# Two-layer transformer block on one core: scores from split bf16 operands against fp32 scores on 32-row groups of TensorE

## Time and profile before

| | us |
|---|---|
| median of three runs | 294.47 (289.23 to 296.59) |
| the profiled execution | 290.26 |
| its span on the core | 288.4 |
| PE busy | 208.4 (72%) |
| DVE busy | 187.2 (65%) |
| ACT busy | 118.9 (41%) |
| POOL busy | 83.0 (29%) |
| mean granted clock of TensorE | 0.846 of 2.4 GHz |

### The profile page before, as it was taken

How to read it: one execution, slowest core, us unless ns; L and a number is a source line. 1 busy time by engine, 2 the same in 40 slices (tenths; PEclk the granted TensorE clock), 3 DMA queues, 4 the chain that set the end, 5 groups by cost and what they waited for, 6 DMA issues and landing times.

```text
span 288.4 us, 4749 instructions
## 1 busy us (share of the span) xinstructions
PE 208.4 (72%) x1541; PEld 153.4 (53%) x1541; DVE 187.2 (65%) x545; ACT 118.9 (41%) x265; POOL 83.0 (29%) x110
## 2 busy tenths in 40 slices
PE   2812776745978697948878797866985978782996
PEld 1512654624757466736557575543764755261683
DVE  4656875148885885488776945678578566715763
ACT  2510565516576361325783622353563421341220
POOL 1402675328054321123371312050512021001000
PEclk9965599765699999795899997978699999586699
DMA  4562712204001210220002200200020002000000
GB/s 118 173 159 74 273 39 65 52 16 92 2 4 46 71 50 0 50 61 0 3 18 64 64 18 0 56 18 2 4 53 5 0 2 60 16 4 0 0 0 18
DMA packets 21895, 12.61 MB, mean 44 GB/s; under 512 B 2966, under 2 KB 20998, under 8 KB 21878
## 3 DMA queue, kind: packets, MB, share of 16 engines
q1 hardware_dynamic: 20790, 11.88, 15.3%
q10 hardware_dynamic: 1088, 0.52, 0.7%
HBM read 5.44 MB, written 0.54 MB: 21 GB/s over the span
## 4 chain that ended last, share of the span: by engine, by line
PE 34%; DVE 27%; issue 14%; POOL 7%; ACT 6%; DMA 5%; SPq 5%; DVEq 0%; POOLq 0%; ACTq 0%
PE bank L1104 6%; PE bank L1124 5%; PE bank L1059 5%; DVE mx L731 3%; DVE xn L709 3%; POOL rstd L372 3%; PE bank L1045 3%; ACT pt L551 3%; POOL es L413 3%; DVE ct L750 3%; SPq L255 2%; SPq L258 2%; DVE es L721 2%; PE bank L1013 2%; DVE stats L697 2%
## 5 line engine op out<-in xcount | busy, mean ns | idle before, releaser
L413 POOL TENSOR_TENSOR es<-es,mx 128x512 f32<-128x512 f32 x32 | 33.3, 1053 | 38.5 <-DVE mx L716 38.1
L1034 PE MATMUL bank<-ident,es 128*128 128x128 f32 x128 | 25.2, 345 | 10.4 <-ACT es L539 10.2
L372 POOL TENSOR_TENSOR rstd<-ve,half 128x2 f32<-128x2 f32 x16 | 11.2, 698 | 67.7 <-DVE ve L703 67.3
L539 ACT ACTIVATE es<-es 128x512 f32<-128x512 f32 x32 | 19.0, 626 | 27.4 <-POOL es L413 27.3
L583 ACT ACTIVATE gth<-bank 128x256 f32<-128x256 f32 (+1 forms) x36 | 13.4, 380 | 37.7 <-PE bank L1104 37.7
L1034 PEld LDWEIGHTS bank<-ident,es 128*128 128x128 f32 x128 | 19.1, 179 | 14.2 <-ACT es L539 13.7
L1104 PE MATMUL bank<-xnT,wg 128*128 128x256 f32 (+1 forms) x72 | 25.7, 441 | 0.6 <-DVE gb L836 0.4
L721 DVE TENSOR_TENSOR es<-bank,biasq 128x512 f32<-128x512 f32 x32 | 21.2, 684 | 7.5 <-PE bank L1018 7.4
L1059 PE MATMUL bank<-pt,va 128*32 128x128 f32 x512 | 25.0, 292 | 0.0
L830 DVE SCALAR_TENSOR_TENSOR ga<-gth,bank 128x256 f32<-128x256 f32 (+1 forms) x36 | 15.0, 416 | 14.6 <-ACT gth L583 14.1
L1104 PE MATMUL bank<-xnT,wu 128*128 128x256 f32 (+1 forms) x72 | 23.2, 406 | 0.0
(11 more groups left out here) (131 smaller groups left out, 394.0 us busy)
## 6 DMA issues: line engine op xcount, KB each, us to landing
kst<-ksp SPq DMA_DIRECT2D x24, 64.0 KB, 2.6
qst<-qsp SPq DMA_DIRECT2D x48, 32.0 KB
kst<-ksp SPq DMA_DIRECT2D x48, 32.0 KB
qst<-qsp SPq DMA_DIRECT2D x24, 64.0 KB, 2.6
biasq<-rel_bias_scratch SPq DMA_DIRECT2D x2, 512.0 KB, 4.7
wg<-in_wg SPq DMA_DIRECT2D x1, 544.0 KB, 4.1
wu<-in_wu SPq DMA_DIRECT2D x1, 544.0 KB, 5.4
wd<-in_wd SPq DMA_DIRECT2D x1, 512.0 KB, 5.6
```

Of the source, the lines that this page charges most:

```text
L372: pool.tensor_tensor(rstd[:, n, :], ve[:, n, :], half[:, 0:2], ALU.pow).then_inc(sem(f"rstd{n}"), 1)
L413: pool.tensor_tensor(es[:, b, h], es[:, b, h], mx[:, 0, b, h].unsqueeze(2).broadcast_to([128, 4, SEQ]), ALU.subtract).then_inc(sem(f"less0 ...
L1034: ins = pe.transpose(dst[:, s * SEQ:(s + 1) * SEQ], es[:, b, 4 * c + s], ident[:])
```

## The change

- q and k stay fp32. `qf` and the new `km` hold them for both layers and all four pairs. The splits, the stacks and their DMAs, `ones`, the clearing of the stacks, and GpSimd's subtractions are gone.
- A group is now four heads, 32 rows of the projection in the reference's own order. `project_k` writes four copies of k, each scaled by a column of `kmask` that is one on one head's 8 rows of a group and zero elsewhere. `scores` is one fp32 product for a group: 32 rows, 128 stationary columns (queries), 512 moving columns (the keys of four masked copies). The group's 32 rows choose the row group of the array, and groups go to the two banks of ring "s" in turn.
- `scores1_turned` has four fp32 products with 32 rows for a group, and four bf16 products with `maxsel`, which pick a head's three maximum parts out of `nmT`, now laid out by 32 partitions a group. The DMA of `max_rows` is gone.
- `values` sends its four heads of a group to four column groups. Wo's rows are ordered to suit.
- Three small copies on VectorE ("tiny"), which only carried a wait, are gone. Turns 1 and 2 are written out on every engine. Two small inputs are loaded besides, `kmask` and `maxsel` (128 KB).

```diff
-        qsp = sb("qsp", [128, 3, 2, TOK], BF16)
-        qst = [sb("qst0", [SROWS, HALF, 2, TOK], BF16), sb("qst1", [MROWS, HALF, TOK], BF16)]
-        kst = [sb("kst0", [SROWS, HALF, TOK], BF16), sb("kst1", [MROWS, HALF, 2, TOK], BF16)]
+        qf = sb("qf", [128, 2, PAIRS, TOK])
+        km = sb("km", [128, 2, PAIRS, GH, TOK])
...
             def project_k(l, p, turn):
                 src = read(act, "m", f"k{l}", turn)[:, 0:TOK]
-                if l == 0:
-                    act.activation(ksp[:, 0, 0], src, ACT.Identity, bias=bias)
-                free(act.activation(kf[:, l], src, ACT.Identity, bias=bias), "m", f"k{l}", turn)
+                for h in range(GH):
+                    ins = act.activation(km[:, l, p, h], src, ACT.Identity, bias=bkm[:, l, h:h + 1],
+                                         scale=kmask[:, h:h + 1])
+                free(ins, "m", f"k{l}", turn)
...
             def scores(l, b, cs, p, turn):
...
                 for c in cs:
                     dst = fill(pe, "s", f"S{l}{b}{c}", turn)
-                    for hp in (2 * c, 2 * c + 1):
-                        at = 2 * (hp - 2 * c) * SEQ
-                        if l == 1:
-                            ins = pe.matmul(dst[:, at:at + 2 * SEQ].rearrange("p (h k) -> p h k", h=2),
-                                            qst[1][0:SROWS, hp, tok], kst[1][0:SROWS, hp, :, tok],
-                                            start=True, stop=True)
-                        else:
-                            for hh in range(2):
-                                ins = pe.matmul(dst[:, at + hh * SEQ:at + (hh + 1) * SEQ],
-                                                qst[0][:, hp, hh, tok], kst[0][:, hp, tok], start=True, stop=True)
+                    g = slice(32 * c, 32 * c + 32)
+                    filled(pe.matmul(dst[:].rearrange("p (h k) -> p h k", h=GH), qf[g, l, p, tok], km[g, l, p, :, tok],
+                                     start=True, stop=True), "s", f"S{l}{b}{c}", turn)
...
             def scores1_turned(b, p, turn):
-                after(pe, f"max1{b}_in", p, of=16)
+                freed(pe, "m", f"nmT1{b}", turn)
                 for c in range(4):
                     dst = fill(pe, "t", f"T1{b}{c}", turn)
-                    for s in range(4):
-                        hp, hh = 2 * c + s // 2, s % 2
-                        ins = pe.matmul(dst[:, s * SEQ:(s + 1) * SEQ], kst[1][:, hp, hh, tok],
-                                        qst[1][:, hp, tok], start=True, stop=True)
+                    g = slice(32 * c, 32 * c + 32)
+                    for h in range(GH):
+                        pe.matmul(dst[:, h * SEQ:(h + 1) * SEQ], km[g, 1, p, h, tok], qf[g, 1, p, tok],
+                                  start=(h == 0), stop=False, skip_group_check=True)
+                    for h in range(GH):
+                        ins = pe.matmul(dst[:, h * SEQ:(h + 1) * SEQ], maxsel[g, h].bitcast(BF16), nmT[g, b],
+                                        start=False, stop=True, skip_group_check=True)
                     filled(ins, "t", f"T1{b}{c}", turn)
...
             def values(l, b, p, turn):
-                    for s in range(4 * c, 4 * c + 4):
-                        head = HALF * (s % 2) + s // 2
-                        j, g = head // 4, head % 4
-                        ins = pe.matmul(dst[32 * j:32 * j + VW, g * SEQ:(g + 1) * SEQ], va[:, l, b, head],
-                                        pt[:, l, b, s], start=True, stop=True)
+                    for s in range(4):
+                        ins = pe.matmul(dst[32 * s:32 * s + VW, c * SEQ:(c + 1) * SEQ], va[:, l, b, 4 * c + s],
+                                        pt[:, l, b, 4 * c + s], start=True, stop=True)
...
             def variance(n, src, p):
-                dve.tensor_copy(dummy[:, 1:2], half[:, 0:1]).then_inc(sem("wait_carried"), 1)
...
-            with pe.Fori(1, PAIRS - 1) as i:
+            for i in range(1, PAIRS - 1):
                 body(i)
```

More of the change, by code:

```diff
@@ L308, in _ @@
             sp.wait_ge(sem("stored"), 16)
-            for hh in range(2):
-                src = bass.AP(tensor=rel_d.tensor, offset=HALF * hh * (REL + 1),
+            for g in range(2):
+                src = bass.AP(tensor=rel_d.tensor, offset=HALF * g * (REL + 1),
                               ap=[[1, SEQ], [REL + 1, HALF], [1, SEQ]])
[L313 to L316, removed]
+                sp.dma_start(biasq[:, HALF * g:HALF * (g + 1), :], src).then_inc(sem("biasq_in"), 16)
+            sp.dma_start(maxsel[:], maxsel_d).then_inc(sem("maxsel_in"), 16)
             after(sp, "res0", 0)
             load_pair(sp, 1)
[L320 to L324, removed]
             def store(p, first):
@@ L470, in body @@
                 residual(2, xs[2])
-                rest_q(1, i, i)
-                last_q(1, i)
             body(0)
-            with pool.Fori(1, PAIRS - 1) as i:
+            for i in range(1, PAIRS - 1):
                 body(i)
@@ L632, in body @@
                     softmax1(0, i)
-                if not last:
-                    middle_k(0, i + 1)
-                    middle_q(0, i + 1)
                 if not first:
@@ L653, in body @@
                 copy_turned(xnT[1][:], "xn1T", i)
-                if not last:
-                    top_k1(i + 1, i)
                 gelu(0, i)
@@ L659, in body @@
                     copy_comb(i)
-                if not last:
-                    middle_k(1, i + 1)
                 if not first:
@@ L674, in _ @@
             body(0)
-            with act.Fori(1, PAIRS - 1) as i:
+            for i in range(1, PAIRS - 1):
                 body(i)
@@ L944, in _ @@
             body(0)
-            with dve.Fori(1, PAIRS - 1) as i:
+            for i in range(1, PAIRS - 1):
                 body(i)
@@ L1249, in _ @@
             body(0)
-            pe.wait_ge(sem("kst_ones"), 32)
+            pe.wait_ge(sem("maxsel_in"), 16)
             pe.wait_ge(sem("moe_in"), 64)
             pe.wait_ge(sem("expsel"), 1)
-            with pe.Fori(1, PAIRS - 1) as i:
+            for i in range(1, PAIRS - 1):
                 body(i)
@@ L1282, in _, with max_selector, key_masks @@
             down(ECH, p, "tail")
+def max_selector():
+    out = np.zeros((GROUPS, 32 // GH, GH, GH, SEQ), np.uint16)
+    for h in range(GH):
+        out[:, 0:3, h, h] = 0x3F80
+    return out.reshape(128, GH, SEQ)
+def key_masks():
+    out = np.zeros((GROUPS, GH, DK, GH), np.float32)
+    for h in range(GH):
+        out[:, h, :, h] = 1.0
+    return out.reshape(128, GH)
 def bucket_onehot():
```

140 lines of the change are left out of this document (32 added, 108 removed).

## The result

The changed kernel took 373.2 us (median of four executions, 370.5 to 376.1) against 292.6 us for the kernel before (289.2 to 296.6). Ratios here leave out executions over 1.5% above the fastest of their kernel; this one is 1.281, 95% interval 1.265 to 1.296: slower by 80 us. The direction was forecast, with a chance of 0.53 for slower; the size was not: 301 us was predicted, with a range that ended at 318. The profiled execution took 376.1 us, with a span of 374.3 and a mean granted clock of 0.685; the other three had 0.69 to 0.74.

What follows compares the result with a forecast made beforehand. Hand-overs bound the kernel, TensorE having least to spare. Terms summed to +13.9 us at the present clock, +3.3 at a lifted one; the middle, +8.6 on 290.3, gave 298.9, plus half of 4.2: 301 us, range 286 to 318.

Steps and rivals of the forecast that it cites:

- Plain scores: Score products: neighbouring groups run side by side, 0.86 us for two warm; one product 1.76 cold.
- Rival A: Scores and turned scores: row groups do not run together, about 320 us; chance 0.15.
- Turned scores: Turned scores: two groups at once and two banks, a batch 4.2 us against 2.6; +1.6 warm, +3.5 cold.
- The clock: Whole kernel: +13.9 us if the clock stays, +3.3 if added products lift it; the middle, +8.6, taken.
- rival B: Attention: the clock falls where it is high now, doubling turned scores and transposes; +5 us a turn, 315; chance 0.10.
- Rival C: Low-clock stretches of turns and tail: more TensorE work lifts the clock, giving 286 us; chance 0.20.
- my +3.3 for the warm case: Whole kernel: the sum of all terms if the added products lift the clock in the low-clock stretches, +3.3 us.
- Setup: Setup: 1.97 us wait goes, cold first product takes 1.3 longer, bias lands perhaps 0.5 earlier; -1.0 us.
- Values: Value products: four column groups instead of two, a call from 1.54 to 1.07 us; -0.6 for a pair.
- The sum of turn 2: Turn 2: transposes of 148.94 come 5.1 us later, then -0.6, -0.4, -0.3 and -0.4; net +3.4.
- Turns written out and small copies: Turns: writing out saves -0.4 us per looped turn, dropping VectorE's small copies about -0.3 a turn.
- the cover named for its nine copies: ScalarE before the turned maxima: nine copies, 4.1 us, hidden by TensorE's slower scores; without that +1.8 us a turn.

Runs made afterwards that it cites:

- the run with one row group: The changed kernel with all four plain score groups reading rows 0 to 31; 407.1 us, ratio 1.392 to the kernel before.
- Mending the clock alone: Two runs of the changed kernel: 128 rows in plain and turned scores, 330.5 us; 128 rows in the plain scores alone, 322.6 us.
- the order alone: The changed kernel with the turned scores of two neighbouring groups issued alternately; 357.0 us, ratio 1.221 to the kernel before.
- together 43: The changed kernel with 128 rows in the plain scores and turned scores of neighbouring groups issued alternately on 32 rows; 330.0 us, ratio 1.125.

## Why the prediction was wrong

*What bounds it:* right that TensorE had least to spare, and that ScalarE paced the turned scores. After the change TensorE paces both.

*Plain scores:* the step "so tiles of the array do run at once; I take side by side" was right, at the price given: 2.08 us for two groups at the low clock against 1.76 and the drain. At the high clock two groups took 1.13 us (0.86 and the drain). Rival A is excluded for them by the run with one row group.

*Turned scores:* this step failed: "with two groups at once and two banks, one batch is ... 4.2 us". The groups overlap only at the seam, since all fp32 products of one stand ahead of the next in the queue. I had read from the earlier trace rows that tiles run at once and carried it over without asking for the order: in `values` two column groups alternate, here nothing alternates. From its first product to the end of its last exponential, the measure of the prediction, a batch took 8.75 us (177.44 to 186.19) at the low clock, where 6.1 was priced: 2.6 more for each of eight batches, 21 us. Alternating two groups gave 16 of them back. At the high clock, with 128 rows in the plain scores, a batch took 5.1 where 4.2 was priced. The rule of the Trainium skill on weight loads (TensorE: Matmul & The Clock Gate, Part 3), which I had weighed and set aside, does not hold in this trace either: loads of 0.32 us on average pass beside products of the same row group that follow each other every 0.21 us.

*The clock:* this step failed too, and it is the larger failure. The sum was placed between "if the clock stays as it is" and "if the added products lift the clock"; its fall stood only as rival B, with a chance of 0.10 and +5 us a turn. B's mechanism is what happened, and B was priced too low. Turn 2 grew by 20.9 us against my net +3.4 (the order's loss is in it), as the low clock also slowed projections, value products and plain scores over 44 to 55 us of each of turns 1 to 3, not only the two parts that I had priced. Rival C's argument, more work for TensorE and so a higher clock, is refuted: TensorE is busy 97% of a stretch at half clock. Mending the clock alone takes off 43 to 51 us, the order alone 16; together 43, as the clock falls again in part.

*What stays:* with the clock at 0.935 the kernel is still 29 us behind. TensorE has more to do: plain scores 66.6 us where both forms took 29.7 before, turned ones 33.8 and 12.5 (in part beside each other) where they took 12.9.

```profile
L1018 PE MATMUL bank<-kst,qst 96*128 96x128 bf16 x128 | 14.0, 257 | 5.3 <-DVE es L721 2.8 <-DMA qst<-qsp 2.0 <-DVE mx L731 0.4
L1045 PE MATMUL bank<-qst,kst 102*128 102x128 bf16 x128 | 12.9, 245 | 5.2 <-ACT pt L551 3.2 <-DMA qst<-nmT_sb 1.5
```

But part of this is the price of the 128 rows themselves, which end the overlap: two groups of plain scores take 1.88 us, where 32 rows at the high clock took 1.13. No run has the changed kernel's own products at the high clock throughout, so my +3.3 for the warm case was not put to the test. How the 29 us divide was not separated.

*Setup:* -1.0 was wrong. The bias did not land sooner without the stacking traffic; VectorE's masking add began at 18.18 instead of 17.48, and the first add at 27.38 instead of 27.33. The 1.97 us wait went, so that the first scores start at 25.16 instead of 26.61. VectorE's first add stands 2.2 us behind their start instead of 0.7: the cold fp32 product costs 1.5 (1.3 priced).

*Values:* right in the kernel before: about -7 us measured for -5. In the changed kernel one call at the high clock took 1.18 us (1.07 priced) and one at the low clock 1.94. *The sum of turn 2:* its terms come to 4.9, not 5.1, a slip that changes nothing. *Turns written out and small copies:* -5 measured for -2 priced. *DMAs gone:* layer 1's scores had waited 0.3 us in all for a stacking DMA, so there was next to nothing to gain in the turns, as priced; no run takes the DMAs out alone.

*ScalarE:* the cover named for its nine copies held: TensorE was later still.

## What to carry to other kernels

Price a product by its columns at both clocks, and ask which clock its form will leave behind: 32 rows instead of 128 (or of 96 and 102) cost 43 us on one kernel and 12 on the other by the row count alone. Row groups help only where neighbours in the program stand in different ones. A mend that makes TensorE wait can lose what it saves when the clock falls behind the wait.

## What was not expected of the hardware

- With products on 32 rows the granted clock stood at 0.50 for 55 and 44 us at a stretch with TensorE busy 93% and 97% of it; with 64 rows it was 0.51 over 44 us with TensorE busy all the time; with the plain scores on 128 rows it was 1.00 in the like stretch. How the chip comes to this the runs do not show; only the row count was varied, at 32, 64 and 128.
- Turned scores on 32 rows did not lower the clock so long as plain scores used 128 rows (0.935 over the span). With a pause of 1.26 us between their pairs it fell to half for seven microseconds.
- A product in another row group can start ahead of products that stand before it in the program: at 179.31 us against 179.42.
- Row groups run side by side in fp32 as well: 68.9 us against 112.6 for the same 128 passes.
